# Maxima of the first attention unit's last two key chunks taken as one tile plus the relu of a difference, with the negated queries on ScalarE's side and three value projections moved later

## The chip, the cores and the metric

The kernel runs on one core of a Trainium2 chip. The metric is the device time of one execution in microseconds, as the median of three runs. Engines are named PE (TensorE), DVE (VectorE), ACT (ScalarE), POOL (GpSimd) and SP (SyncE, here only a queue that issues DMAs).

## The reference

Two transformer layers on 2048 tokens of width 128, each an attention and a feed-forward part behind a modulated layer norm. The change touches only the attention of the first layer, whose core is:

```python
q = (x @ Wq.T + bq).reshape(b, s, 16, 8)          # s = 2048, 16 heads of 8
k = (x @ Wk.T + bk).reshape(b, s, 16, 8)
v = (x @ Wv.T + bv).reshape(b, s, 16, 8)
w = jnp.einsum('bshd,bzhd->bhsz', q, k) / jnp.sqrt(8)
w = jax.nn.softmax(w, axis=-1)                    # subtracts each row's maximum over all 2048 keys
vw = jnp.einsum('bhsz,bzhd->bshd', w, v)
x = x + ga * (vw.reshape(b, s, 128) @ Wo.T + bo)
```

Behind it come the routed feed-forward part of layer 0, and layer 1 with causal attention over 8 heads of 16 and a gated mixing step.

## The kernel before

**Staging.** Layer 0's attention runs in 16 units, layer 1's in 8. A unit of layer 0 is one chunk of 512 queries (`CH`) and one quad of 4 heads. It has two parts. The first makes the row maxima: for each of 4 query tiles `qt` (128 queries), 2 pairs of heads `pair` and 4 key chunks `kb` of 512 keys, one score tile `s` is made, 32 in all. PE writes the pair's two halves of 128x512 into a double bank, `S0` and `S1` in turn (L985, two matmuls of 24 rows each, since q and k are held as three half-precision parts of 8). DVE reduces the 128x1024 numbers to two maxima in `mx` (L1377) and gives the bank back. When a unit's 32 tiles are done, DVE takes the maximum over the four chunks and negates it (`neg`, `nm`, L1385), POOL splits it in two half-precision parts (L1925 to L1929), PE turns it (`neg_turn`, L1008), ACT copies it to `nrow` (L1622), and four DMAs put it as two more rows beside the queries (L2078).

The second part needs these rows: for each of 16 tiles of 128 keys (a step), PE makes the transposed scores with the maximum subtracted (`st`, L1024, 26 rows, banks `T0` to `T2` in turn), ACT takes the exponential (L1637) and PE multiplies by the values (`pv`, L1059). In the steady state the score tiles of the next unit are made beside the steps of the present one, two tiles a step.

**The first unit** has nothing before it to hide behind. Its score tiles run in the order of the key chunks (`score_tiles`: `kb` outermost), since the chunks of k are still being projected, split into parts, written to DRAM and loaded back in the other layout (`project`, `split`, `load`; stores L2037 and L2038, loads L2051, all issued by SP in the order written). Call these tiles 0 to 31: tile 16 is the first of chunk 2, tile 24 the first of chunk 3. Then come seven tiles of unit 1, and only then the first step. Between the tiles PE does the remaining projections of q (L943), the modulation `mod` (L889, twelve matmuls of one column), the value projections `values` (L965, four of them, each copied by ACT at L1605 into `Va`), and matmuls of ones whose result nobody reads, `keep_busy` (L912).

**What sets the order.** `make_plan` writes one list of stages by hand and by rules; every engine walks this list and does what concerns it, in that order, with semaphore waits. `next_t` deals out `T0`, `T1`, `T2` in turn, `next_s` deals out `S0`, `S1`. A bank is opened by PE only when its last reader has freed it. `rows_in` makes PE wait for the loads of the k and q chunk. ACT's queue is strictly in order too: a `split` of q needs the shared buffer `qf` and its parts, which are free only when the DMAs that store an earlier chunk's parts are done.

## Time and profile before

| what | value |
|---|---|
| three runs | 1031.02, 1036.03 and 1037.11 us, median 1036.03 |
| profiled execution, its own time | 1036.88 us |
| its span from the first to the last instruction | 1035.1 us |
| mean granted clock of PE | 0.964 of full speed |
| busy, PE / DVE / ACT / POOL | 965.8 / 876.2 / 810.9 / 220.6 us |
| chain that ended last | PE 53%, DVE 30%, ACT 6% |
| largest line of that chain | DVE mx L1377, 26% of the span |

The profile is one execution. "Busy" adds up instructions, and the busy time of PE is modelled, since matmuls are pipelined. Two instructions of one kind may overlap by some 80 ns in it, so the pace of a row of them is read from their starts. A row of the timeline may merge several like instructions: it gives the first start, the time from there to the last end, and the count. The granted clock is the share of 2.4 GHz at which PE was let run: 1.00 or 0.50 (1.2 GHz).

### The profile page before, as it was taken

To read this page: it belongs to the slowest core of one execution; us is meant where nothing else is said; L and a number is where in the kernel's file an instruction comes from. 1 tells how busy PE (TensorE), PEld (TensorE's weight loads), DVE (VectorE), ACT (ScalarE), POOL (GpSimd) and SP (SyncE) were. 2 spreads that over 40 slices of the span, in tenths; PEclk is the share of its full clock that TensorE was granted. 3 is DMA by queue.
4 is the path that set the end of the run, shared out by engine and by line. 5 is a ranking of instruction groups with operands and counts; after the bars stand their busy time and mean duration, and the time that the engine had idled before them with its cause. 6 is when DMAs were issued, how large, how long until landed. Compare 5 with 4: busy or idle time off the path is not lost.

```text
span 1035.1 us, 23103 instructions
## 1 busy us (share of the span) xinstructions
PE 965.8 (93%) x9342; PEld 363.7 (35%) x9342; DVE 876.2 (85%) x1123; ACT 810.9 (78%) x1627; POOL 220.6 (21%) x395
## 2 busy tenths in 40 slices
PE   5999999999999999999999799989998999888988
PEld 2542322233333333333333145423333464332324
DVE  7999999999999999999999788853578777889704
ACT  4149999998999988999998588765774577667886
POOL 4233300003121103221203400141032312301112
PEclk9889999999999999999999789987899999999999
DMA  3520400000000000000000263112100441100000
GB/s 102 172 54 3 138 17 17 2 2 2 2 2 2 2 2 2 1 3 2 2 2 2 70 196 94 41 38 56 37 3 1 122 112 43 47 12 2 1 12 11
DMA packets 41387, 37.05 MB, mean 36 GB/s; under 512 B 5085, under 2 KB 39453, under 8 KB 41281
## 3 DMA queue, kind: packets, MB, share of 16 engines
q1 hardware_dynamic: 39024, 30.20, 10.1%
q0 software_dynamic: 1824, 5.25, 1.8%
q8 instruction: 73, 1.20, 0.5%
q14 instruction: 34, 0.27, 0.1%
q10 hardware_dynamic: 432, 0.13, 0.1%
HBM read 21.92 MB, written 13.30 MB: 34 GB/s over the span
## 4 chain that ended last, share of the span: by engine, by line
PE 53%; DVE 30%; issue 7%; ACT 6%; POOL 2%; DMA 1%; another core or an unknown queue 0%; ACTq 0%; DVEq 0%; POOLq 0%; SPq 0%
DVE mx L1377 26%; PE O L1059 20%; PE T L1024 11%; ACT PT L1637 2%; PE S L993 2%; PE T L1138 2%; PE T L1035 2%; PE S L985 1%; ACT PT L1631 1%; PE S L1189 1%; POOL XP L1994 1%; PE S L998 1%; PE T L943 1%; PE O L912 1%; PE T L1145 1%
## 5 line engine op out<-in xcount | busy, mean ns | idle before, releaser
L1377 DVE TENSOR_REDUCE mx<-S 128x2 f32<-128x1024 f32 (+2 forms) x672 | 755.1, 1179 | 56.6 <-PE S L998 21.3
L1637 ACT ACTIVATE PT<-T 128x512 f32<-128x512 f32 (+2 forms) x1280 | 657.8, 585 | 96.3 <-PE T L1024 41.1
L1059 PE MATMUL O<-PT,Va 128*9 128x256 f32 (+1 forms) x4040 | 337.2, 395 | 4.5 <-ACT Os L1671 4.5
L1024 PE MATMUL T<-Qs,Ks 26*128 26x512 f16 x1024 | 242.9, 394 | 11.9 <-ACT PT L1637 6.3
L985 PE MATMUL S<-Ks,Qs 24*128 24x512 f16 x1024 | 202.7, 394 | 8.1 <-DVE mx L1377 6.0
L1024 PEld LDWEIGHTS T<-Qs,Ks 26*128 26x128 f16 x1024 | 68.0, 91 | 232.1 <-issue 136.3
L1059 PEld LDWEIGHTS O<-PT,Va 128*9 128x9 f32 x4040 | 67.6, 88 | 125.4 <-issue 111.0
L1059 PE MATMUL O<-PT,V 128*17 128x256 f32 (+2 forms) x984 | 83.3, 406 | 1.2 <-ACT Os L1671 0.9
L993 PE MATMUL S<-K,Qs 48*128 48x512 f16 (+3 forms) x320 | 60.1, 359 | 11.7 <-DVE mx L1377 9.8
L985 PEld LDWEIGHTS S<-Ks,Qs 24*128 24x128 f16 x1024 | 48.2, 91 | 31.8 <-DVE mx L1377 24.9
L1035 PE MATMUL T<-Qs,K 50*128 50x512 f16 (+3 forms) x256 | 51.0, 356 | 5.3 <-ACT PT L1637 3.9
L1825 POOL TENSOR_SCALAR_AFFINE_SELECT PT<-PT 128x256 f32<-128x256 f32 x64 | 26.3, 418 | 119.4 <-ACT PT L1637 92.8
L1925 POOL TENSOR_SCALAR n<-nm 128x16 f16<-128x16 f32 x24 | 6.4, 265 | 175.1 <-DVE nm L1385 174.9
L1977 POOL TENSOR_TENSOR gates<-gates 128x256 f32<-128x256 f32 x16 | 11.6, 727 | 136.3 <-ACT gates L1723 136.3
L1938 POOL TENSOR_TENSOR vw<-om,rl 128x128 f32<-128x128 f32 x16 | 6.5, 406 | 128.4 <-DVE rl L1391 128.4
L1035 PEld LDWEIGHTS T<-Qs,K 50*128 50x128 f16 x256 | 14.2, 93 | 44.9 <-issue 27.9
L1059 PEld LDWEIGHTS O<-PT,V 128*17 128x17 f32 x984 | 16.8, 95 | 35.0 <-issue 26.4
L1631 ACT ACTIVATE PT<-S 128x1024 f32<-128x1024 f32 (+3 forms) x32 | 27.7, 945 | 1.2 <-PE S L1035 1.2
L993 PEld LDWEIGHTS S<-K,Qs 48*128 48x128 f16 x320 | 15.8, 94 | 34.8 <-DVE mx L1377 24.1
L1622 ACT ACTIVATE nrow<-T 8x512 f16<-8x512 f16 x24 | 14.0, 584 | 12.8 <-PE T L1008 12.4
L1994 POOL DMA_INDIRECT XP<-sorted_y,posu x16 | 16.3, 1017 | 36.1 <-DMA sorted_y<-Vf 31.9
L1340 DVE RECIPROCAL rl<-O 128x4 f32<-128x4 f32 x3 | 0.5, 183 | 24.1 <-PE O L1095 24.0
(338 smaller groups left out, 892.8 us busy)
## 6 DMA issues: line engine op xcount, KB each, us to landing
Wg<-in_L_ffn_experts SPq DMA_DIRECT2D x28, 192.0 KB, 2.6
Ks<-in_L_ffn_experts SPq DMA_DIRECT2D x20, 192.0 KB, 2.9
Vf<-sorted_x SPq DMA_DIRECT2D x12, 256.0 KB, 4.6
sorted_y<-Vf SPq DMA_DIRECT2D x12, 256.0 KB, 2.3
rows_q<-q SPq DMA_DIRECT2D x7, 256.0 KB, 2.4
sorted_x<-XP POOLq DMA_DIRECT2D x1, 1792.0 KB, 10.7
Qs<-nrow SPq DMA_DIRECT2D x96, 2.0 KB
Qs<-rows_q SPq DMA_DIRECT2D x8, 192.0 KB, 3.7
```

The lines of the kernel that those rows point to most:

```text
L985: m = e.matmul(two[:, i, :], Qs[r0:r0 + 24, quad, q0:q0 + 128], Ks[r0:r0 + 24, quad, CH * kb:CH * kb + CH], start=True, stop=True, tile_po ...
L993: m = e.matmul(two[:, i, 0:n], Q1[r0:r0 + 48, 2 * quad + pair, q0:q0 + 128], K1[r0:r0 + 48, CH * kb:CH * kb + n], start=True, stop=True, t ...
L1024: e.matmul(bank, Ks[r0:r0 + 26, quad, keys], Qs[r0:r0 + 26, quad, CH * c:CH * c + CH], start=True, stop=True, tile_position=(r0, 0)).then_ ...
L1035: m = e.matmul(bank[:, lo:CH], K1[r0:r0 + 50, keys], Q1[r0:r0 + 50, 2 * quad + pair, CH * c + lo:CH * c + CH], start=True, stop=True, tile ...
L1059: m = e.matmul(acc[32 * g:32 * g + d1, lo:hi], v, PT[(2 * j + g // 2) % 4][:, p0 + lo:p0 + hi], start=fresh, stop=True, skip_group_check=n ...
L1138: e.matmul(bank[:, 0:256], w[:, 128 * bl:128 * bl + 128], hc(c, 256 * half, 256 * half + 256), start=True, stop=True).then_inc(full, 1)
L1377: e.tensor_reduce(mx[:, u % 2, h0:h0 + 2, kb], two[:, :, 0:n], AX.X, ALU.max).then_inc(free, 1)
L1622: e.activation(nrow[:, U % 2, :], bank.bitcast(F16)[0:8, 0:CH], ACT.Copy).then_inc(free, 1)
L1631: e.activation(both, Sb[turn["st", L, j, 2 * pair][0]][:, :, lo:CH], ACT.Exp).then_inc(free, 1)
L1637: e.activation(PT[(2 * j + pair) % 4][:, CH * i + lo:CH * i + CH], bank[:, lo:CH], ACT.Exp).then_inc(free, 1)
L1825: e.affine_select(out=both, in_=both, compare_op=ALU.is_ge, fill=0.0, base=0, pattern=[[0, 2], [1, 128]], channel_multiplier=-1).then_inc( ...
L1994: e.indirect_dma_start(out=XP[:, t, :], out_offset=None, in_=sorted_y[g], in_offset=off(posu[:, t:t + 1])).then_inc(y_gathered[c], 16)
```

## The change

Only unit 0 is concerned (`FOLDED`). For each of its 8 pairs of `qt` and `pair`:

- the tile of chunk 3 is no longer made or reduced, so unit 0 has 24 score tiles, and the former tiles 24 to 31 are gone;
- a new stage `fold`, one for each head, makes on PE the difference of the scores of chunk 3 and chunk 2 in a `T` bank, by two accumulating matmuls on the same 24 rows: negated queries times chunk 2, plus queries times chunk 3. ACT writes the relu of it to SBUF (`relus`, four buffers of 128x2x512 in `Vf`);
- the tile of chunk 2 (tiles 16 to 23) is then not reduced by one instruction of 128x1024 but by two `tensor_tensor_reduce` of 128x512, which add tile and relu and take the maximum of the sum. max(a, b) = a + relu(b - a);
- chunk 1's reduction (tiles 8 to 15) reads the same 128x1024 numbers but writes two maxima for each head, over 256 keys each, so that the fourth column of `mx` is filled too.

A stage `negate` makes the negated queries by one ACT copy behind tile 12. A tile's two folds stand two tiles ahead of it in the list from tile 14 on. `mod` moves from behind tile 18 to behind tile 16, `values(0)` from behind tile 25 to behind tile 19, and `values(1)`, `(2)`, `(3)` from between the last tiles of unit 0 to behind the first, second and seventh tile of unit 1. Behind tiles 14 to 21 `keep_busy` has 2 matmuls where it had 8 or 4; in the section of unit 1 it has 6 in three places where it had 10. Nothing behind the first step moves on any engine, and SP and POOL keep their order throughout.

```diff
+FOLDED = {0: [(qt, pair) for qt in range(4) for pair in range(2)]}
...
-        return [(qt, pair, kb) for qt, kb in pairs for pair in (1, 0)]
+        return [(qt, pair, kb) for qt, kb in pairs for pair in (1, 0) if kb < 3 or (qt, pair) not in FOLDED.get(u, ())]
...
+        if is_folded(t):
+            for i in range(2):
+                fold(t, i)
         between("s", *t)
+        for t2 in tiles[si[0]:si[0] + (4 if u else 2)]:
+            if is_folded(t2) and t2 not in seen:
+                seen.add(t2)
+                for i in range(2):
+                    due.append(lambda t2=t2, i=i: fold(t2, i))
...
-        elif i == 18:
+        elif i == 16:
             beside("mod", 1)
-        elif i in (25, 27, 29, 31):
-            values((i - 25) // 2)
-        if 4 <= i < 25:
-            keep_busy(4 if i in (5, 7, 9, 11, 13, 15, 18) else 8)
+        elif i == 19:
+            values(0)
+        if i == 12:
+            negate(0)
+        if i >= 14:
+            while due:
+                due.pop(0)()
+        if 4 <= i < 22:
+            keep_busy(4 if i in (5, 7, 9, 11, 13) else 8 if i < 14 else 2)
     for i in range(7):
...
         emit_s()
+        if i in (0, 1, 6):
+            values(i + 1 if i < 2 else 3)
...
-        keep_busy(3 if i in (3, 4, 5) else 10 if i < 6 else 10)
+        keep_busy(3 if i in (3, 4, 5) else 6 if i in (0, 1, 6) else 10)
...
+                elif name == "fold":
+                    u, qt, pair, i = a
+                    c, quad = UNITS[0][u]
+                    bank, full = opened(("fold",) + tuple(a))
+                    rows_in(c, quad, 2)
+                    rows_in(c, quad, 3)
+                    pe.wait_ge(negated, P.negated[u])
+                    r0 = 64 * pair + 32 * i
+                    q0 = CH * c + 128 * qt
+                    e.matmul(bank, negs[r0:r0 + 24, u % 2, 128 * qt:128 * qt + 128], Ks[r0:r0 + 24, quad, 2 * CH:3 * CH], start=True, stop=False,
+                             tile_position=(r0, 0))
+                    e.matmul(bank, Qs[r0:r0 + 24, quad, q0:q0 + 128], Ks[r0:r0 + 24, quad, 3 * CH:4 * CH], start=False, stop=True,
+                             tile_position=(r0, 0)).then_inc(full, 1)
...
+                    if L == 0 and (qt, pair) in FOLDED.get(u, ()) and kb == 2:
+                        r = relus[P.folds[u, qt, pair] % 4]
+                        for i in range(2):
+                            done(("fold", u, qt, pair, i))
+                            m = e.tensor_tensor_reduce(r[:, i, :], two[:, i, :], r[:, i, :], 1.0, -3.0e38, ALU.add, ALU.max, mx[:, u % 2, h0 + i, 2:3])
+                        m.then_inc(free, 1)
+                        continue
+                    if L == 0 and (qt, pair) in FOLDED.get(u, ()) and kb == 1:
+                        e.tensor_reduce(mx[:, u % 2, h0:h0 + 2, 1:4:2], two[:, :, :].rearrange("p h (s n) -> p h s n", s=2), AX.X, ALU.max).then_inc(free, 1)
+                        continue
...
+                elif name == "fold":
+                    u, qt, pair, i = a
+                    bank, free = filled(("fold",) + tuple(a))
+                    n = P.folds[u, qt, pair]
+                    if n >= 4:
+                        u0, qt0, pair0 = fold_keys[n - 4]
+                        done(("s", 0, u0, qt0, pair0, 2))
+                    e.activation(relus[n % 4][:, i, :], bank, ACT.Relu).then_inc(free, 1)
+                elif name == "negate" and a[0] == 0:
+                    done(("pick", "q"))
+                    e.activation(negs[:, 0, :], Qs[:, 0, 0:CH], ACT.Copy, scale=-1.0).then_inc(negated, 1)
```

Three places show what moves. On PE, before, from tile 14 (the first row) to tile 16 (the last); T2 takes the second half of the q projection of chunk 3, and O the matmuls of ones:

```order
L985 MATMUL S0<-Ks,Qs 128x512 x2
L912 MATMUL O<-onesb 128x128 x8
L985 MATMUL S1<-Ks,Qs 128x512 x2
L943 MATMUL T2<-hT,wqT 128x256
L912 MATMUL O<-onesb 128x128 x4
L985 MATMUL S0<-Ks,Qs 128x512 x2
```

On PE, with the change, from the second fold of tile 16 (T1), which stands behind tile 14, to tile 16 (the last row); `Vf` holds the negated queries:

```order
L1052 MATMUL T1<-Ks,Vf 128x512
L1054 MATMUL T1<-Ks,Qs 128x512
L955 MATMUL O<-onesb 128x128 x2
L1028 MATMUL S1<-Ks,Qs 128x512 x2
L986 MATMUL T2<-hT,wqT 128x256
L1052 MATMUL T2<-Ks,Vf 128x512
L1054 MATMUL T2<-Ks,Qs 128x512
L1052 MATMUL T0<-Ks,Vf 128x512
L1054 MATMUL T0<-Ks,Qs 128x512
L955 MATMUL O<-onesb 128x128 x2
L1028 MATMUL S0<-Ks,Qs 128x512 x2
```

The folds of tile 17 now stand between the projection into T2 and tile 16, and the first of them is the next user of T2.

On ACT, before, the splits of the q chunks 2 (T1) and 3 (T2) and the first copy of values:

```order
L1596 ACTIVATE qf<-T1,bqs,sc 128x512
L1598 ACTIVATE q3<-qf 128x512
L1596 ACTIVATE qf<-T2,bqs,sc 128x512
L1598 ACTIVATE q3<-qf 128x512
L1605 ACTIVATE Va<-O 128x64x8
```

On ACT, with the change, the same place; `Vf<-Qs` is the negation and `Vf<-T0` and its like are relus:

```order
L1662 ACTIVATE qf<-T1,bqs,sc 128x512
L1664 ACTIVATE q3<-qf 128x512
L1791 ACTIVATE Vf<-Qs 128x512
L1788 ACTIVATE Vf<-T0 128x512
L1788 ACTIVATE Vf<-T1 128x512
L1662 ACTIVATE qf<-T2,bqs,sc 128x512
L1664 ACTIVATE q3<-qf 128x512
L1788 ACTIVATE Vf<-T2 128x512
L1788 ACTIVATE Vf<-T0 128x512
```

The relus of tile 16 stand ahead of the split of q chunk 3, those of tile 17 and all later ones behind it.

On PE at the end of the section of unit 1, before, from its fifth tile (the first row, S0) to the first step (T1 from `Ks` and `Qs`):

```order
L985 MATMUL S0<-Ks,Qs 128x512 x2
L898 MATMUL T2<-XP 128x128 x2
L912 MATMUL O<-onesb 128x128 x3
L985 MATMUL S1<-Ks,Qs 128x512 x2
L904 MATMUL T0<-XP 128x128 x2
L912 MATMUL O<-onesb 128x128 x3
L985 MATMUL S0<-Ks,Qs 128x512 x2
L912 MATMUL O<-onesb 128x128 x22
L1024 MATMUL T1<-Qs,Ks 128x512
```

With the change, from the sixth tile (S1) to the first step (T2):

```order
L1028 MATMUL S1<-Ks,Qs 128x512 x2
L947 MATMUL T1<-XP 128x128 x2
L955 MATMUL O<-onesb 128x128 x3
L1028 MATMUL S0<-Ks,Qs 128x512 x2
L1008 MATMUL T2<-wvT,hT 128x128 x4
L955 MATMUL O<-onesb 128x128 x18
L1080 MATMUL T2<-Qs,Ks 128x512
```

A value projection now stands ahead of the first step, and four of the twenty-two matmuls of ones are gone.

## Rows read from the trace of the kernel before

**Rows 1.** Busy time by window: stretch, length, busy us (instructions) by engine, clock, DMA.

```profile
20.00:40.00 20.00, 17.81 (x140) 9.77 (x141) 18.88 (x17) 7.11 (x11) 7.28 (x8) 1.00 0.50 160
40.00:60.00 20.00, 18.73 (x134) 12.27 (x131) 17.80 (x20) 3.38 (x6) 1.39 (x2) 0.74 0.28 87
...
110.00:200.00 90.00, 88.56 (x968) 26.51 (x960) 89.86 (x88) 86.23 (x169) 10.95 (x47) 1.00 0.16 46
```

**Rows 2.** Timeline, DVE in the first unit: start, us, instruction, count, idle before.

```profile
25.74 17.06 DVE L1377 TENSOR_REDUCE mx<-S 128x2 f32<-128x1024 f32 x15 [0.49 <-PE S L985]
...
53.63 6.88 DVE L1377 TENSOR_REDUCE mx<-S 128x2 f32<-128x1024 f32 x6 [1.32 <-PE S L985]
```

**Rows 3.** Timeline, DVE at the end of unit 0 and in unit 1.

```profile
60.54 0.22 DVE L1385 TENSOR_REDUCE nm<-mx 128x16 f32<-128x64 f32 x1
60.68 8.00 DVE L1377 TENSOR_REDUCE mx<-S 128x2 f32<-128x1024 f32 x7
...
68.86 5.75 DVE L1377 TENSOR_REDUCE mx<-S 128x2 f32<-128x1024 f32 x5 [0.17 <-PE S L985]
```

**Rows 4.** Busy time by window, the two low stretches of PE's clock.

```profile
44.40:54.40 10.00, 10.00 (x59) 6.37 (x59) 7.84 (x7) 0.60 (x1) 0.00 (x0) 0.50 0.26 76
...
71.00:72.00 1.00, 0.73 (x8) 0.22 (x10) 1.00 (x2) 0.86 (x2) 0.99 (x1) 0.76 0.92 327
72.00:73.00 1.00, 1.00 (x12) 0.11 (x4) 1.00 (x2) 0.00 (x0) 0.92 (x2) 0.50 1.12 328
...
74.00:75.00 1.00, 1.00 (x16) 0.24 (x12) 0.80 (x2) 0.57 (x2) 0.80 (x1) 0.53 0.39 66
```

**Rows 5.** DVE by line and shape: out<-in, count, busy us, mean ns, idle before.

```profile
L1441 DVE TENSOR_TENSOR Vf<-S,Vf 128x512 f32<-128x512 f32 x8 | 5.5, 691 | 0.5 <-PE S L1131 0.3
```

**Rows 6.** Timeline, ACT: an accumulator read between two activations, and exponentials.

```profile
6.02 0.19 ACT L1576 ACTIVATION_READ_ACCUMULATOR squares<-wkT 128x1 f32 x1
6.12 0.29 ACT L1576 ACTIVATE squares<-wqT 128x128 bf16<-128x128 f32 x1
...
77.10 12.94 ACT L1637 ACTIVATE PT<-T 128x512 f32<-128x512 f32 x24
```

**Rows 7.** Timeline, SP's queue and ACT around tile 16.

```profile
34.73 2.43 SPq L2051 DMA_DIRECT2D Ks<-rows_k  x6
...
37.63 0.47 SPq L2038 DMA_DIRECT2D rows_q<-q  x1
...
40.30 0.78 ACT L1596 ACTIVATE qf<-T,bqs,sc 128x512 f32<-128x512 f32 x1 [4.82 <-DMA rows_q<-q]
```

**Rows 8.** Timeline, PE: two fp16 matmuls of 512 columns, and what follows.

```profile
18.02 0.59 PE L958 MATMUL S<-PT,Vf 128*128 128x512 f16 x2
...
18.45 0.60 PE L930 MATMUL T<-idf,xh 128*128 128x128 f32 x4
```

**Rows 9.** Timeline, PE: `mod`; then tile, ones and values at half clock.

```profile
40.91 1.50 PE L889 MATMUL T<-cs,XP 128*128 128x1 f32 x12
...
45.91 0.61 PE L985 MATMUL S<-Ks,Qs 24*128 24x512 f16 x2
...
46.45 1.03 PE L912 MATMUL O<-onesb 128*128 128x128 bf16 x8
...
50.97 2.08 PE L965 MATMUL O<-wvT,hT 128*128 128x128 f32 x8
```

**Rows 10.** Timeline, PE: last value projection, then the end of unit 1's section.

```profile
58.62 1.16 PE L965 MATMUL T<-wvT,hT 128*128 128x128 f32 x8
...
59.72 0.39 PE L985 MATMUL S<-Ks,Qs 24*128 24x512 f16 x2
...
66.55 0.39 PE L985 MATMUL S<-Ks,Qs 24*128 24x512 f16 x2
...
66.87 1.40 PE L912 MATMUL O<-onesb 128*128 128x128 bf16 x22
...
68.21 0.40 PE L1024 MATMUL T<-Qs,Ks 26*128 26x512 f16 x3
```

More of the change, by code:

```diff
@@ L362, in make_plan @@
     out = dict.fromkeys(units, 0)
-    urgent = []
+    urgent, due, seen = [], [], set()
     si = [0]
@@ L379, in may_score, with is_folded, negate, fold @@
         return may_begin(*tiles[si[0]][:2])
+    def is_folded(t):
+        return t[0] == 0 and t[4] == 2 and t[2:4] in FOLDED.get(t[1], ())
+    def negate(u):
+        if u in FOLDED:
+            P.negated[u] = len(P.negated) + 1
+            P.stage("negate", u)
+    def fold(t, i):
+        key = t[1:4] + (i,)
+        if ("fold",) + key in P.turn:
+            return False
+        if i == 0:
+            P.folds[t[1:4]] = len(P.folds)
+        beside("fold", *key)
     def emit_s():
@@ L483, in do_later @@
     def do_later():
+        if due:
+            due.pop(0)()
+            return
         if urgent and urgent[0][0] <= now[0]:
@@ L739, in adaln_two_layers @@
         bsg, bt = Vf[:, 5632:5632 + CH], Vf[:, 6144:6144 + CH]
+        negs = Vf[:, 256:768].bitcast(F16).rearrange("p (k n) -> p k n", k=2)
+        relus = [Vf[:, o:o + 2 * CH].rearrange("p (i n) -> p i n", i=2) for o in (768, 1792, 5632, 6656)]
         pick = Vf[:, 0:256].bitcast(F16).rearrange("p (k s m) -> p k s m", k=2, s=2)
```

27 lines of the change are left out of this document (25 added, 2 removed).

## The prediction

> **What bounds the kernel now.** I read the busy times by window first. From 20 to 40 us DVE is busy for 18.88 us of 20, and in the steady state, 110 to 200 us, for 89.86 of 90, with PE at 88.56 and ACT at 86.23; in the first unit ACT has little to do, 3.38 us of the 20 behind 40 us [rows 1]. So ACT can take relus there, and whatever makes DVE end its share of the first unit earlier moves all that follows, since DVE has no free time behind it in which the gain could be lost.
>
> The timeline of DVE gives the pace: fifteen reductions in 17.06 us, 1.137 us each from start to start; the first of them is tile 4, so tile 15 starts at 38.25 and tile 16 at 39.39 [rows 2]. The last tile of unit 0 ends at 60.51 and `neg` starts at 60.54, the seven tiles of unit 1 follow at 1.143 each, and the eighth starts at 68.86 after only 0.17 us without work [rows 3]. The sixteen tiles that the change touches thus take from 39.39 to 60.54, 21.15 us, where sixteen times 1.137 is 18.2. The other 3 us are waits: PE ran at half its clock from 44.4 to 54.4, and DVE was busy for 7.84 of these 10 us only [rows 4].
>
> **What it removes and adds on DVE.** Sixteen reductions go, 18.2 us. Sixteen reduce-of-sum instructions of 128x512 come. The trace has none. Nearest is the sum of a PSUM and an SBUF source of 128x512 in single precision, 691 ns [rows 5]; a reduction of 1024 shows about 1.22 us where its pace is 1.137, so I take 0.61 as the pace. The order lists a second instruction behind each, which writes the accumulator. On ACT such a read takes 0.19 us, and the next instruction starts 0.10 after it [rows 6]; I take 0.10. A pair then costs 2 x 0.71 = 1.42 us, eight pairs 11.4. Bounds: with the read hidden 1.22 a pair; and at half rate, each half as dear as a whole reduction of 1024 plus the read, 2 x 1.24 = 2.48. I stay near the lower, since the row of the same two sources shows full rate. The reductions of chunk 1 keep their 1024 elements, and cost the same.
>
> A page of the Trainium skill speaks against the change here: Vector Engine (DVE) Microarchitecture Reference, Points that are easy to get wrong, says that the instruction family with two sources and an accumulator runs at half throughput if both sources are wider than bf16 and in SBUF. Here one source is in PSUM, so by its letter it does not apply; if it did, the sum would be that of the third rival. No row before has the accumulator.
>
> **What it adds on ACT and PE.** Sixteen relus of 128x512, each like the exponential of that size: 24 of them in 12.94 us, 0.54 each [rows 6]. A tile's two relus, 1.1 us, lie beside DVE's 1.42, and ACT was idle there. ScalarE: Activation LUTs, Rules for kernel authors, in the Trainium skill, would have a relu on VectorE; here VectorE is the engine that is waited for, and the trace disagrees with that advice.
>
> PE gets four matmuls of 512 columns for a tile. Two fp16 matmuls of that size took 18.02 to 18.45, 0.43 us [rows 8]: 0.86 for the two folds, and less if the two heads' row groups overlap. With the tile itself at 0.32 (66.55 to 66.87) and two ones at 0.06 each (22 in 1.40 us) PE needs 1.30 a tile at full clock [rows 10], under DVE's 1.42. At half clock the tile takes 0.54, the folds 1.72, the ones 0.26: 2.52 us [rows 9], far over it.
>
> **What is late next.** Two waits of the new folds lie on DVE's path.
> First, tile 16's folds stand ahead of tile 15 and need chunk 3 of k. Its four loads are the fifth to eighth of the twelve; the seventh starts at 34.73, the eighth is issued by 35.5. A store issued from 37.63 to 38.10 released ACT at 40.28, 2.2 us after its issue [rows 7]; so the rows are in at 37.7. Then 0.86 + 0.12, and tile 15 is issued at 38.7 and reduced from 39.1, 0.8 late.
> Second, and larger: tile 17's first fold needs bank T2, which holds the q projection of chunk 3 until ACT has read it, and ACT could start this only at 40.30, when the store had landed (0.78 us, to 41.08) [rows 7]. SP's order is unchanged, so that time stays. PE stands from about 39.7 to 41.1, and tile 16 is queued behind these folds: 41.1 + 0.98 = 42.1, its scores are in at 42.5. DVE's first pair starts at 42.5 instead of 39.39, 3.1 us late; the first wait is hidden in this.
> Then comes `mod`, 1.50 us on PE [rows 9], and tile 18's folds, ahead of tile 17: 42.4 + 1.5 + 0.98 = 44.9, scores at 45.3. Pair 16 ended at 43.9, so 1.4 us are lost, in which the copies of `mod` lie. Tiles 18 and 19 are issued at 46.2 and 47.5, in time. The value projection behind tile 19 takes 1.10 (58.62 to 59.72) [rows 10]; tile 20 is issued at 47.5 + 1.10 + 1.30 = 49.9 and its pair, due at 49.6, starts at 50.3: 0.7 lost.
>
> At full clock unit 0 would end at 42.5 + 11.4 + 1.4 + 0.7 = 56.0.
>
> **The clock.** The granted clock fell to half at 44.4, two us behind `mod`, whose matmuls have a single column, and came back at 54.4 [rows 4, 9]. With the change the same `mod` has a standstill of 1.4 us ahead of it, so I expect it to fall again. How long it stays low the rows show twice: 10 us, and some 3.4 us at 71.5 to 75 (0.24/0.5 + 2 + 0.94) [rows 4]. I take one short stretch: 3.4 us hold 1.35 tiles of 2.52 instead of 2.4 pairs of 1.42, 1.5 us lost, less 0.2 for PE's lead: 1.3. Unit 0 ends at 57.3, against 60.54: 3.2 us earlier.
>
> **Behind it.** Before, the first step came at 68.21, 7.7 behind the end of unit 0. The last tile of unit 1 waits for DVE as before, 6.0 behind; then 0.32, a value projection 1.10 and 18 ones 1.1 where 22 ones took 1.3 to 1.4: 8.5 [rows 10]. The first step and the eighth tile come 0.8 later relative to `neg`, and DVE, which had 0.17 us free [rows 3], stands for it. The other two value projections replace ones in a section that waits for DVE's 1.143 a tile, and cost nothing; without that cover 1.1 each. The copies on ACT lie in idle time.
>
> **Sum:** 3.2 - 0.8 = 2.4 us less. From the profiled execution's 1036.88 us that is 1034.5; its time is 0.85 above the median of the three runs, 1036.03, which would give 1033.6. I say 1034.
>
> **The rivals.**
> 1. *Larger gain.* The accumulator read costs nothing and the two heads' matmuls overlap (8 x 0.20 = 1.6), the clock stays up (1.3), and the ones at the end are covered by the DMAs of the maxima (0.8): 2.4 + 3.7 = 6.1 us, 1030.8. For it: PE is denser in the folds than it was with the ones. Against it: the standstill ahead of `mod`.
> 2. *Slower, because PE takes the bound at half clock.* If the clock is down from 44.4 to 54.4 as before, tiles 18 and 19 are issued at 47.4 and 49.9, tile 20 behind the values (2.0 [rows 9]) at 54.4, its pair starts at 55.0, and four pairs end at 60.7. With the 0.8 behind it the kernel is 1.0 us slower, 1037.9. If the clock stays down to the end of the unit, three more tiles at 2.52, a last 0.6 and a pair give 64.0: 4.3 us slower, 1041.2. It decides from about 8 us of low clock on, where 1.1 us lost a tile have eaten the gain. For it: that stretch before was that long, with PE at 10.00 of 10.00 us [rows 4]. Against: the second one was short.
> 3. *The reduce-of-sum runs at half rate.* Eight pairs of 2.48 from 42.5, with 0.3 for tile 17: 62.6, 2.1 later, and 0.8: 1039.8.
> 4. *It does nothing.* The end of the section is set by something that does not move, the rows of the maxima or the late loads behind them: these follow `neg` in SP's queue, so they move with it, and I give this little. 1036 to 1037.
>
> **How the numbers follow.** Forecast as above, 1032.5 to 1036.0: 0.50. Rival 1, 1029 to 1032.5: 0.20. Rival 2: 0.20. Rival 3: 0.05. Rival 4: 0.05. The three runs before already spread over 6 us, so the measured median adds 1 us either way. From 1029 to 1039 leaves out the far ends of rivals 1 to 3 and some of that spread, 2 in 10 at most; the likeliest case alone is 1032 to 1036.5. One per cent is 10.4 us, about what can be told from no change. Even pairs of 1.22 us without any wait behind the one for T2 would end unit 0 at 42.5 + 9.8 = 52.3, 8.2 us earlier, and miss it; the worst rival is at +5. So within 1%: 0.96, and 0.02 on each side for a state of the chip that no row shows.
>
> **What would show it.** Reduce-of-sum 0.65 to 0.75 us with a read behind it, a pair every 1.4 us; the first pair at 42.5, with PE waiting for T2 and ACT for the store of q; a granted clock of 0.50 for about 3.4 us within 43 to 50; `neg` at 57.3; the first step 8.5 behind it; from there on the same distances as before, and a span shorter by what `neg` gained less 0.8. It is wrong if the first pair starts near 39.4, if `neg` comes behind 60.5, or if a pair takes over 1.6 us.

## The result, and the profile after

The changed kernel takes 1043.9 us (median of 16 runs, 1037.6 to 1056.3), the kernel before 1037.0 in the same series (16 runs, 1031.0 to 1043.1): a ratio of 1.0071, with an interval of 1.0048 to 1.0094. It is slower by 0.7%, where I had said 1034 us and a range to 1039. The profiled execution took 1043.28 us, its span is 1041.5, and its mean granted clock 0.951 where that of before was 0.964. A ratio here and below leaves out a kernel's runs that lie over 1.5% above its fastest (one of the changed kernel's sixteen, and up to seven of twelve further down), while a median takes all of them, so the two can differ.

VectorE's timeline of the changed kernel (start, us, instruction, shapes, count, idle before and who ended it) answers [rows 2, 3]:

```profile
42.77 0.69 DVE L1437 CUSTOM_DVE_ANT_0 Vf<-S,Vf 128x512 f32<-128x512 f32 x1 [3.35 <-PE S L1028]
43.38 0.08 DVE L1437 DVE_READ_ACCUMULATOR2_ANT mx<- 128x1 f32 x1
43.38 0.69 DVE L1437 CUSTOM_DVE_ANT_0 Vf<-S,Vf 128x512 f32<-128x512 f32 x1
...
47.25 0.69 DVE L1437 CUSTOM_DVE_ANT_0 Vf<-S,Vf 128x512 f32<-128x512 f32 x1 [1.34 <-PE S L1028]
...
48.97 0.69 DVE L1437 CUSTOM_DVE_ANT_0 Vf<-S,Vf 128x512 f32<-128x512 f32 x1 [0.41 <-PE S L1028]
...
54.53 0.69 DVE L1437 CUSTOM_DVE_ANT_0 Vf<-S,Vf 128x512 f32<-128x512 f32 x1 [2.53 <-PE S L1028]
...
60.54 0.22 DVE L1451 TENSOR_REDUCE nm<-mx 128x16 f32<-128x64 f32 x1
...
63.17 1.23 DVE L1443 TENSOR_REDUCE mx<-S 128x2 f32<-128x1024 f32 x1 [1.28 <-PE S L1028]
...
66.48 2.36 DVE L1443 TENSOR_REDUCE mx<-S 128x2 f32<-128x1024 f32 x2 [2.08 <-PE S L1028]
...
102.53 0.22 DVE L1451 TENSOR_REDUCE nm<-mx 128x16 f32<-128x64 f32 x1
```

The first pair starts at 42.77 and then DVE waits for PE ahead of almost every pair. The maxima of unit 0 (`nm`) come at 60.54, to the hundredth where they came before [rows 3]: all that the folds save is eaten. Behind them stand two waits for unit 1's tiles, 1.28 and 2.08 us, where before seven tiles ran without one [rows 3].

PE's timeline shows why. The first rows are the last q projection (L986), first matmuls of folds (L1052) and `mod` (L932) in unit 0, then come the value projections (L1008), the ones (L955), the turned maxima (L1064, the transposition that unit 0's rows of maxima wait for) and the first step (L1080):

```profile
37.92 0.70 PE L986 MATMUL T<-hT,wqT 128*128 128x256 f32 x2
40.83 0.61 PE L1052 MATMUL T<-Ks,Vf 24*128 24x512 f16 x2 [2.20 <-ACT qf L1662]
...
42.66 2.72 PE L932 MATMUL T<-cs,XP 128*128 128x1 f32 x12
...
47.00 0.63 PE L1052 MATMUL T<-Ks,Vf 24*128 24x512 f16 x2
...
48.72 0.63 PE L1052 MATMUL T<-Ks,Vf 24*128 24x512 f16 x2
...
59.88 2.08 PE L1008 MATMUL T<-wvT,hT 128*128 128x128 f32 x8
61.74 0.85 PE L955 MATMUL O<-onesb 128*128 128x128 bf16 x6
...
63.06 1.54 PE L1008 MATMUL O<-wvT,hT 128*128 128x128 f32 x8
65.29 0.51 PE L955 MATMUL O<-onesb 128*128 128x128 bf16 x6 [0.69 <-ACT Va L1671]
65.73 0.39 PE L1064 MATMUL T<-idb,n 128*8 128x128 f16 x4
...
72.83 0.40 PE L1080 MATMUL T<-Qs,Ks 26*128 26x512 f16 x3
```

And the granted clock (window, its length, busy us and count of PE, PE's loads, DVE, ACT and POOL, clock, DMA share, GB/s), to set against [rows 4]:

```profile
39.00:40.00 1.00, 0.00 (x0) 0.00 (x0) 0.41 (x1) 0.01 (x1) 0.00 (x0) 1.00 0.65 171
40.00:41.00 1.00, 0.17 (x2) 0.13 (x4) 0.00 (x0) 0.97 (x2) 0.00 (x0) 0.50 0.77 258
...
63.00:64.00 1.00, 1.00 (x7) 0.94 (x6) 0.83 (x1) 0.00 (x0) 0.00 (x0) 0.56 0.00 0
64.00:65.00 1.00, 0.60 (x6) 0.41 (x4) 0.40 (x1) 0.36 (x1) 0.00 (x0) 1.00 0.00 0
```

The clock falls at 40.0, in the standstill that waits for bank T2, and comes back at 63.9: 23.9 us at half, where it was 10.2 in the profile of before. In that stretch a tile with its folds costs PE 1.72 us (47.00 to 48.72), more than the 1.22 of DVE's pair. The turned maxima come at 65.73 instead of 61.86, the first step at 72.83 instead of 68.21 [rows 10], and the maxima of unit 1 at 102.53 instead of 97.83: 4.7 us late. From the trace of before:

```profile
61.86 0.38 PE L1008 MATMUL T<-idb,n 128*8 128x128 f16 x4
```

```profile
97.83 0.22 DVE L1385 TENSOR_REDUCE nm<-mx 128x16 f32<-128x64 f32 x1
...
563.84 0.22 DVE L1385 TENSOR_REDUCE nm<-mx 128x16 f32<-128x64 f32 x1
...
615.92 0.22 DVE L1385 TENSOR_REDUCE nm<-mx 128x16 f32<-128x64 f32 x1
```

Up to unit 9 the lag stays within 4.4 and 4.7 us. But it does not reach the end unchanged. These are the maxima of units 13 and 14 in the changed kernel, beside the last two rows above:

```profile
571.22 0.22 DVE L1451 TENSOR_REDUCE nm<-mx 128x16 f32<-128x64 f32 x1
...
615.83 0.22 DVE L1451 TENSOR_REDUCE nm<-mx 128x16 f32<-128x64 f32 x1
```

The lag is 7.4 us at unit 13 and gone at unit 14, and at all maxima from there up to 765 us the two kernels lie within 0.7 us of each other. The 6.4 us between 1043.28 and 1036.88 come behind that, where low stretches of the clock differ again (17.1 us from 777 on in the change, 3.4 in before). So this one pair of profiles shows what the change does to the first unit and to unit 1, and can't show that this is what the medians differ by; for that see the timed runs below.

### The profile page after: what moved, and what is told of

Its sections match the earlier page's. It is cut to its first block, busy times and chain, and to the rows that moved or that the text cites. A ratio compares the mean times of both kernels' runs of the same rounds, so it can differ in the third digit from the quotient of the medians.

```text
span 1041.5 us, 23027 instructions
## 1 busy us (share of the span) xinstructions
PE 972.2 (93%) x9282; PEld 362.7 (35%) x9282; DVE 868.2 (83%) x1139; ACT 820.4 (79%) x1644; POOL 220.7 (21%) x395
## 4 chain that ended last, share of the span: by engine, by line
PE 55%; DVE 27%; issue 7%; ACT 6%; POOL 2%; DMA 2%; SPq 1%; ACTq 0%; DVEq 0%; POOLq 0%
DVE mx L1443 23%; PE O L1115 20%; PE T L1080 11%; PE S L1036 2%; ACT PT L1703 2%; PE T L1091 2%; PE T L1194 2%; PE S L1028 1%; ACT PT L1697 1%; PE S L1245 1%; PE S L1041 1%; POOL XP L2089 1%; PE S L1186 1%; PE T L986 1%; PE T L1201 1%
## 5 line engine op out<-in xcount | busy, mean ns | idle before, releaser
L1443 DVE TENSOR_REDUCE mx<-S 128x2 f32<-128x1024 f32 (+2 forms) x648 | 727.2, 1176 | 59.5 <-PE S L1041 23.4
L1080 PE MATMUL T<-Qs,Ks 26*128 26x512 f16 x1024 | 241.2, 394 | 4.0 <-ACT PT L1703 2.1
L1080 PEld LDWEIGHTS T<-Qs,Ks 26*128 26x128 f16 x1024 | 67.6, 91 | 222.3 <-issue 129.3
```

Of the source, the lines that this page charges most:

```text
L1080: e.matmul(bank, Ks[r0:r0 + 26, quad, keys], Qs[r0:r0 + 26, quad, CH * c:CH * c + CH], start=True, stop=True, tile_position=(r0, 0)).then_ ...
L1443: e.tensor_reduce(mx[:, u % 2, h0:h0 + 2, kb], two[:, :, 0:n], AX.X, ALU.max).then_inc(free, 1)
```

## The experiments

My two reasons were the half clock (theory C in the expectations: the standstill loses the clock and PE then bounds) and the value projections put ahead of the turned maxima (theory V). All sixteen further runs stand in this table: the low stretches of the clock that begin before 76 us (each widened to whole microseconds), the starts of unit 0's maxima, of the first step and of unit 1's maxima in the profiled execution, then the median and the ratio to the kernel before on the same chip. Runs with the same first letter shared a chip and the runs of before made there, whose medians were 1046.6 (e), 1044.4 (f), 1038.2 (g), 1045.2 (h) and 1044.5 (i); the first row and the second are the pair of the result.

| kernel | low, us | unit 0 | first step | unit 1 | median | ratio (interval) |
|---|---|---|---|---|---|---|
| before | 44-55, 71-75 | 60.54 | 68.21 | 97.83 | 1037.0 | |
| after | 40-64 | 60.54 | 72.83 | 102.53 | 1043.9 | 1.0071 (1.0048-1.0094) |
| e1 other bank | 37-62, 75-79 | 58.44 | 70.83 | 100.57 | 1057.9 | 1.0125 (1.0075-1.0176) |
| e2 more ones | 39-85 | 65.11 | 83.90 | 113.63 | 1059.6 | 1.0162 (1.0108-1.0215) |
| e3 folds only | 40-89 | 65.20 | 79.25 | 110.17 | 1051.9 | 1.0071 (1.0040-1.0102) |
| e4 values only | 41-66 | 61.83 | 74.20 | 103.90 | 1049.0 | 1.0050 (1.0014-1.0087) |
| f1 ones in the wait | 45-74 | 56.76 | 74.44 | 103.49 | 1048.0 | 1.0024 (0.9996-1.0052) |
| f2 held, values late | 43-64 | 60.86 | 72.25 | 101.30 | 1048.4 | 1.0030 (1.0002-1.0058) |
| f3 shallow ones | 40-61 | 61.82 | 69.49 | 98.63 | 1047.0 | 0.9962 (0.9913-1.0012) |
| f4 after again | 39-64 | 60.43 | 72.71 | 102.40 | 1051.2 | 1.0061 (1.0029-1.0094) |
| g1 half folded | 41-55, 58-73, 75-79 | 57.71 | 71.77 | 101.59 | 1040.8 | 1.0023 (0.9995-1.0051) |
| g2 values after the turn | 41-62, 75-79 | 59.30 | 70.64 | 100.39 | 1041.8 | 1.0054 (1.0020-1.0088) |
| g3 before again | 43-61, 74-78 | 61.96 | 69.63 | 99.38 | 1036.6 | 0.9989 (0.9955-1.0023) |
| h1 shallow opening | 41-62, 65-83 | 63.28 | 73.55 | 104.78 | 1049.6 | 1.0038 (1.0000-1.0076) |
| h2 before, more ones | 54-58, 71-75 | 59.00 | 66.67 | 96.44 | 1044.5 | 0.9971 (0.9927-1.0014) |
| h3 half, more ones | 68-72 | 56.18 | 64.72 | 94.36 | 1048.3 | 0.9979 (0.9929-1.0028) |
| i1 = h3 again | none | 56.24 | 64.78 | 93.83 | 1047.2 | 0.9940 (0.9883-0.9997) |
| i2 = h2 again | 69-76 | 58.27 | 65.93 | 96.78 | 1043.0 | 0.9985 (0.9947-1.0022) |

**The change taken apart (e).** e1 turns the banks by one, so that tile 17's folds need not wait for T2:

```diff
+        if i == 15:
+            P.next_t()
         if i >= 14:
             while due:
```

> The changed kernel with one T bank skipped in the deal, so that tile 17's first fold takes T0 and not T2, which the q projection holds until ACT's split at 40.0 us. In the changed kernel PE stood from 38.6 to 40.8 us there, DVE 3.35 us, and the clock went to half at 40.0 and came back at 63.6. Theory C (the loss is PE at half clock, set off by that standstill): without it tile 16 is issued near 39, the clock holds at least past 44, neg comes at 56 to 58 instead of 60.5, the first step at 65 to 68 instead of 72.8; 4 to 8 us faster than the changed kernel, level with the kernel before or better. Theory V (the loss is the value projections that now stand ahead of neg_turn, whatever the clock): neg comes earlier, but neg_turn still comes about 4 us later behind it than before; at most 3 us of gain. Rival: mod alone, 1.5 us of one-column matmuls, takes the clock down a few us later all the same; then the gain is only the 3 us of the standstill.

e2 gives the folded tiles 8 ones instead of 2:

```diff
-            keep_busy(4 if i in (5, 7, 9, 11, 13) else 8 if i < 14 else 2)
+            keep_busy(4 if i in (5, 7, 9, 11, 13) else 8)
```

> The changed kernel with 8 matmuls of ones behind each of tiles 14 to 21 instead of 2. Theory C with too few ones as the reason why the clock stays low: it comes back between 47 and 54 instead of 63.6, the section of unit 1 runs at full clock, the first step comes 3 to 5 us earlier. If the number of ones has nothing to do with it: the clock stays low, each tile costs 6 x 0.13 = 0.8 us more on PE, which is the bound there, neg comes up to 6 us later, at 65 to 67, and the kernel is 4 to 6 us slower than the changed one. Theory V says nothing of the clock; neg_turn is late behind neg by the values in both cases.

e3 has the folds, with the value projections back between the last tiles of unit 0 (behind tiles 17, 19, 21, 23) and unit 1's section as before:

```diff
-        elif i == 19:
-            values(0)
+        elif i in (17, 19, 21, 23):
+            values((i - 17) // 2)
```

> The folds as in the changed kernel, but the four value projections stand inside unit 0, behind tiles 17, 19, 21 and 23, and the section of unit 1 is that of the kernel before, with its 10 and 12 matmuls of ones. Theory V: neg_turn follows neg in 1.4 us again (1.3 before, 5.2 in the change), the first step comes 7.7 behind neg; the two values at half clock cost 2 x 2.0 inside unit 0 instead, the part of them that PE's lead does not cover, so neg at 63 to 66 and the first step at 71 to 73: 0 to 2 us faster than the changed kernel. Theory C: the clock is low through unit 0 all the same, PE is the bound there at 1.72 us a tile, three more values of 2.0 put neg at 66.5 and the first step at 74, 1 to 2 us slower than the changed kernel.

e4 is the kernel before with three value projections moved as the change moves them, and no folds:

```diff
-        elif i in (25, 27, 29, 31):
-            values((i - 25) // 2)
+        elif i == 27:
+            values(0)
...
+        if i in (0, 1, 6):
+            values(i + 1 if i < 2 else 3)
```

> The kernel before, with all 32 tiles reduced as they were, and only the value projections moved: the first behind tile 27, the other three into the section of unit 1 as in the change, with its 6 ones in place of 10. Theory V: neg_turn waits on PE for two projections and, through the ones in bank O, for ACT's copy; at full clock 2 x 1.1 us and some 0.6, less what PE waited for neg anyway (1.3): neg_turn 1.5 to 2 later behind neg, the first step 2 to 3 later, 2 to 3 us slower than the kernel before. Theory C: at full clock the projections fit beside DVE's 1.143 us a tile, so within 1 us of the kernel before. If the clock is low at neg here too, up to 4 slower.

In e1 the standstill is gone, PE is busy throughout 38 to 40 us, and the clock is low all the same, from 37.9 us on and for 23.9 us. So that standstill neither starts the low stretch there nor keeps it up (a wait of 0.48 us for the loads of k is left ahead of 36.6), and C's forecast of a clock held past 44 us failed. The gain of 2.0 us at unit 1's maxima is what V and the rival allowed. e2 and e3 do worse than the change: the clock stays low for 44 and 48 us, through the opening of unit 1. e2 did not bring the clock back sooner with four times the ones, and e3's first step at 79.25 lies 5 us and more behind the forecast of either theory. e4 has unit 1's maxima 6.1 us later than before (4.5 later than g3, a second profile of before) without a single fold. Both parts lose, each alone, though e4's profile has a low stretch of 23.9 us too and so does not price the moved projections at full clock.

The window of e3 behind unit 0, busy PE and yet at half clock:

```profile
56.00:76.00 20.00, 20.00 (x106) 12.04 (x105) 12.53 (x23) 5.64 (x10) 2.03 (x4) 0.50 0.05 10
```

**What the clock follows (f).** Theory S says the standstill, theory D the kind of matmul: the folds and tiles are 24 rows deep, the ones and value projections 128. Theory R says chance. f1 fills the standstill with ones:

```diff
+        if i == 15:
+            keep_busy(32)
         if i >= 14:
             while due:
```

> The changed kernel with 32 more ones matmuls (128 rows deep, some 1.7 us at full clock) put between the last q projection and the folds of tile 17, where TensorE stood still for 2.2 us. Theory S (the standstill costs the clock): TensorE stays at full clock past 43 us, the first unit's negated maxima come at 57 to 58 us instead of 60.5 and the ratio to the kernel before falls to 1.000 or below. Theory D (the folds, only 24 rows deep, in place of ones 128 rows deep cost the clock, whatever the standstill): the clock still falls somewhere in 37 to 48 us and stays low for 20 us or more, the negated maxima come at 60 us or later, ratio 1.005 to 1.015 as before. Theory R (chance of the single run): the low stretch is of any length, the ratio unchanged at 1.007.

f2 adds 6 ones behind each folded tile, and puts the values at tiles 2, 4 and 6:

```diff
-        if i in (0, 1, 6):
-            values(i + 1 if i < 2 else 3)
+        if i in (2, 4, 6):
+            values(i // 2)
```

> As the run with 32 ones in the wait, and besides 6 ones in place of 2 behind each folded tile (full-clock pace 1.26 us a tile against the 1.22 us of the pair), and the three late value projections behind the turned maxima (unit 1's tiles 2, 4 and 6) instead of tiles 0, 1 and 6. Theory S: full clock through the unit, maxima at 57 to 58 us, turned maxima 1.3 us behind them, first step at 65 to 66 us (68.2 before), ratio 0.997 to 0.999. Theory D: the added ones help part of the way; the clock is low for some 10 us as in the kernel before or for over 20; in the second case 1.005 to 1.015. Theory V (the values ahead of the turned maxima): whatever the clock, the turned maxima follow the negated maxima within 2.5 us instead of 5.2, and the ratio falls by about 0.002 to 0.003 against the changed kernel.

f3 is the kernel before with shallow ones in its first unit (a negative count from tile 14 on):

```diff
+                    rows = 128 if n > 0 else 24
-                    for _ in range(n):
-                        e.matmul(BANK[b][:, 0:128], onesb[:, :], onesb[:, :], start=True, stop=True)
+                    for _ in range(abs(n)):
+                        e.matmul(BANK[b][:, 0:128], onesb[0:rows, :], onesb[0:rows, :], start=True, stop=True)
```

> The kernel before, with the 8 or 4 ones matmuls behind each of the first unit's tiles 14 to 24 taken over 24 rows instead of 128: the same columns, the same TensorE time, nothing else changed (these matmuls compute nothing that is used). Theory D (the depth of what TensorE runs is what matters): the low stretch gets longer than the 10 us of before, over 20 us, and the time rises by 0.5 to 1.5%. Theory S and theory R: nothing changes, 1.000 within 0.003.

> The changed kernel once more, for a second profile. Theories S and D: the low stretch of the first unit starts at about 40 us and lasts over 20 us again, the ratio is 1.007. Theory R: it may last 3 to 10 us, with the maxima at 58 us, in this execution.

f4 repeats the change: 23.9 us again, every start within 0.15 us, in both its profiles; theory R loses by that. (The rest of the execution is not repeated: f4's span is 1047.9 us, 6.4 more, with the same first unit.) f1 is the cleanest view of the gain that I had forecast, and of where it goes. DVE's timeline of f1:

```profile
56.76 0.22 DVE L1453 TENSOR_REDUCE nm<-mx 128x16 f32<-128x64 f32 x1
...
63.97 1.23 DVE L1445 TENSOR_REDUCE mx<-S 128x2 f32<-128x1024 f32 x1 [3.35 <-PE S L1030]
```

and PE's between the two:

```profile
59.28 2.08 PE L1010 MATMUL O<-wvT,hT 128*128 128x128 f32 x8
62.05 0.82 PE L957 MATMUL O<-onesb 128*128 128x128 bf16 x6 [0.69 <-ACT Va L1673]
```

The clock holds until 45.9, the mod products take 1.50 us again, and unit 0 ends at 56.76, 3.8 us earlier than before. S had forecast this, but it is not shown to be the reason: the 32 ones are 128 rows deep themselves, e1 lost the clock without that standstill, and D's forecast (a fall within 37 to 48 us, low for over 20) came true as well. Then the clock is low until 73.2, and a value projection of 2.08, half-speed ones and their wait for ACT's copy of bank O turn -3.8 into +5.7 at unit 1's maxima. f2 has the values behind the turned maxima, which come 2.24 us behind unit 0's, as V said. But its unit 0 ends at 60.86, where S said 57 to 58: the clock fell at 43.3, sooner than in f1, in spite of 6 ones for 2, and +3.5 is left at unit 1's maxima.

f3's forecast by theory D was wrong in time: not slower. Its clock was low for 20.5 us. Its window beside that of g3 (the same kernel with deep ones):

```profile
44.00:52.00 8.00, 8.00 (x70) 6.57 (x67) 7.49 (x11) 0.00 (x0) 0.00 (x0) 0.50 0.33 97
```

```profile
44.00:52.00 8.00, 8.00 (x53) 4.84 (x52) 6.88 (x7) 0.00 (x0) 0.00 (x0) 0.50 0.31 93
```

DVE was busy for 7.49 of these 8 us at half clock (6.88 with deep ones): the tiles' matmuls started beside the shallow ones instead of behind them, so PE held up DVE less. With 20.5 us of low clock each, f3's unit 0 ends at 61.82 and h1's (below, with deep ones there) at 63.28. For the clock f3 says nothing: the kernel before can be low for 17.1 us (g3), and in h1, whose code up to the end of unit 0 is that of before, the stretch is 20.5 us, as in f3. Depth of the ones is not shown as the reason for a long low stretch in unit 0.

**Half of it (g).** g1 folds the last two query tiles only, and keeps three value projections in unit 0. Its expectation says that the ones stay at 8, but they do so only up to tile 18; behind tiles 19 to 27 it has none, where before has 8 behind each of 19 to 24:

```diff
-FOLDED = {0: [(qt, pair) for qt in range(4) for pair in range(2)]}
+FOLDED = {0: [(qt, pair) for qt in (2, 3) for pair in range(2)]}
...
-        elif i == 19:
-            values(0)
+        elif i in (19, 23, 25):
+            values((i - 18) // 2 - (i > 19))
...
-        if 4 <= i < 22:
-            keep_busy(4 if i in (5, 7, 9, 11, 13) else 8 if i < 14 else 2)
+        if 4 <= i < 19:
+            keep_busy(4 if i in (5, 7, 9, 11, 13, 15, 16) else 8)
...
-        if i in (0, 1, 6):
-            values(i + 1 if i < 2 else 3)
+        if i == 6:
+            values(3)
```

> Only the last two of the four query tiles (4 of 8 pairs) are folded; the mod products stand behind tile 16 as in the change, the value projections of chunks 0 to 2 stay inside the first unit behind tiles 19, 23 and 25, only that of chunk 3 stands in the second unit (tile 6), and the ones stay at 8. VectorE loses 4 reductions of 1.13 us and has 4 pairs of 1.22 for 4 reductions: 4.2 us less. Theory D with the values (what the shallow folds do to the clock, and three values put ahead of the turned maxima, make the loss): the first unit's maxima come at 57 to 59 us, those of the second unit some 37 to 38 us later, so 95 to 97 us against 97.8 before and 102.5 after the change; ratio 0.996 to 0.999. Theory R (the loss is chance or anywhere else): ratio 1.005 to 1.008 like the change.

g2 is the change with the values at tiles 2, 4 and 6, as in f2, and nothing else.

> The changed kernel with nothing moved but the three late value projections: behind the second unit's tiles 2, 4 and 6 (behind the turned maxima) in place of tiles 0, 1 and 6, with so many ones fewer there. If the values ahead of the turned maxima cost 2.3 us, the first unit's maxima stand at 60.5 us as in the change, the turned maxima within 3 us of them in place of 5.2, the second unit's maxima at 100 to 101 us in place of 102.5, and the ratio is 1.004 to 1.005 in place of 1.007. If their place doesn't matter (they take TensorE's time wherever they stand), the second unit's maxima stay at 102 to 103 us.

> The kernel before, unchanged, for a second profile and as a measure of what two runs of one kernel differ by. Theory D: the first unit's low stretch is short again (3 to 14 us), the maxima come at 60.5 us, the second unit's at 98 us, ratio 1.000 within 0.003. Theory R: the low stretch may be over 20 us here too, with maxima at 61 to 62 us and the second unit's at 100 us or later.

g1 gained 2.8 us in unit 0 and lost it: a second low stretch from 58.5 to 72.2 made the way from unit 0's maxima to the first step 14.1 us, where 7.7 is the rule. The loss moved with the clock, and the forecast of 95 to 97 us missed by 5. g2 shows that the place of the values, ahead of the turned maxima or behind, is a small part. The turned maxima come 2.23 us behind unit 0's (61.53 by PE's timeline, 5.19 in the change), yet unit 1's come 41.1 behind and not 37.3 (42.0 in the change): 0.9 us is the order, the rest is the work itself. It is not the half clock either: in g2 the clock was back at 61.9, and from the turned maxima at 61.53 to the first step at 70.64 it took 9.11 us where before takes 6.35. So three projections in this section cost 2.8 us with PE at full clock for nearly all of it. g3 differs from the first profile of before by 1.5 us in unit 1's maxima, with 17.1 us of low clock against a forecast of 3 to 14, and its own ratio is 0.9989.

**What a low clock costs, by place, and whether more deep work holds it (h, i).** h1 is the kernel before with shallow ones in unit 1's section only; h2 is before with more ones in unit 0; h3 is g1 with more ones. In the last two the edit is the list of counts, first h2's against before, then h3's against the change:

```diff
-            keep_busy(4 if i in (5, 7, 9, 11, 13, 15, 18) else 8)
+            keep_busy(4 if i in (5, 7, 9, 11, 13) else 8 if i < 14 else 6 if i == 15 else 14 if i == 18 else 10)
```

```diff
-        if 4 <= i < 22:
-            keep_busy(4 if i in (5, 7, 9, 11, 13) else 8 if i < 14 else 2)
+        if 4 <= i < 28:
+            keep_busy(4 if i in (5, 7, 9, 11, 13) else 8 if i < 14 else 6 if i == 15 else 14 if i == 16 else 10 if i < 19 else 0 if i in (19, 25) else 4)
```

> The kernel before, with the ones matmuls between the second unit's first seven tiles and the 12 behind them taken over 24 rows instead of 128 (they compute nothing that is used; nothing else changes). Theory P (the price is paid where TensorE bounds: a low clock in the first steps behind the maxima costs, one inside the first unit hardly does): the clock falls between 60 and 80 us, the first unit's maxima stay at 60.5 to 62 us, the second unit's come 40 to 44 us behind them instead of 37.3, ratio 1.003 to 1.008. Rival: the price doesn't depend on the place; with 10 us of low clock more it is 1.003 whichever section, and the distance between the two units' maxima stays below 39 us if the clock holds.

> The kernel before with more ones in the first unit: 10 instead of 8 behind tiles 14 to 24, 6 instead of 4 at tile 15, 14 instead of 4 behind the mod products. If 128-row work keeps the clock: the low stretch of the first unit (10.2 and 17.1 us in the two profiles of before) shrinks to 0 to 7 us, the maxima come at 58 to 60 us, ratio 0.995 to 0.999. If it doesn't, the added ones (0.13 us more a tile at half clock) cost 1 to 2 us: ratio 1.001 to 1.003.

> The half-folded kernel with more ones: 10 behind tiles 14 to 18, 6 at tile 15, 14 behind the mod products, 4 behind the folded tiles and the last ones (none where a value projection stands in their bank). If 128-row work keeps the clock, the second low stretch (58 to 73 us in the half-folded kernel's profile) goes, the first unit's maxima come at 56 to 58 us, the second's at 94 to 97 us, and the ratio is 0.995 to 0.999, better than both kernels. If not, the maxima come at 58 to 60 us and the ratio is 1.002 to 1.006.

> The half-folded kernel with more ones, unchanged, once more. Its first profile had the whole first unit at full clock, maxima at 56.2 us and the second unit's at 94.4 us (97.8 and 99.4 in the two profiles of before), and a ratio of 0.998 with 1 inside its interval. If the first unit's clock is held by the 128-row work, it is held again (low for 0 to 7 us before 75 us), the second unit's maxima come at 94 to 96 us and the ratio is 0.996 to 0.999. If it was chance, 10 to 24 us of low clock stand before 75 us and the ratio is 1.000 to 1.004.

> The kernel before with more ones, unchanged, once more. Its first profile had 3.4 us of low clock in the first unit (10.2 and 17.1 in the two of before) and its ratio was 0.997 with 1 inside its interval. If more 128-row work holds the clock: 0 to 7 us low again, the first maxima at 58 to 60 us, ratio 0.996 to 0.999. If it was chance: 10 to 20 us low, maxima at 61 to 63 us, ratio 1.000 to 1.003.

h1: 17.1 us of low clock behind unit 0's maxima, where before has 3.4, make the distance to unit 1's 41.5 us and not 37.3: 0.31 us for each further microsecond of low clock. That is theory P's forecast for this place. Inside the first unit the price is hardly lower. Up to the end of unit 0 before, g3 and h1 are the same kernel, and their 10.2, 17.1 and 20.5 us of low clock go with maxima at 60.54, 61.96 and 63.28: 0.27 us for each microsecond. So P's contrast between the two places falls.

With more ones the clock is low in unit 0 for 3.4 us (h2), 0 (i2), 0 (h3) and 0 (i1), against 10.2, 17.1 and 20.5 in the three profiles of before's first unit and 13.6 in g1, which has 13.7 more right behind it. That is the clearest effect of the ones here. It is not their number alone: from tile 14 to the end of unit 0 before has 80, h2 110, h3 78, the change 16, and e2 has 64 and f2 80 with low stretches of 44.4 and 20.5 us. h2 and h3 also have 14 ones behind `mod` where before has 4; which of the added ones matter was not tried. h3 and i1 hold the clock through unit 0, i1 up to 241 us. Two windows of i1, and its maxima:

```profile
36.00:56.00 20.00, 18.69 (x176) 11.64 (x173) 17.98 (x32) 7.37 (x13) 1.81 (x3) 1.00 0.41 126
56.00:76.00 20.00, 18.39 (x187) 9.04 (x184) 18.91 (x19) 11.93 (x24) 11.95 (x16) 1.00 0.27 71
```

```profile
56.24 0.22 DVE L1451 TENSOR_REDUCE nm<-mx 128x16 f32<-128x64 f32 x1
...
93.83 0.22 DVE L1451 TENSOR_REDUCE nm<-mx 128x16 f32<-128x64 f32 x1
```

Unit 1's maxima at 94.36 and 93.83, 3.5 to 5.6 us earlier than in the two profiles of before: half folding does gain where PE runs at full clock. At the end nothing certain is left of it. The profile of h3 ends at 1046.0 us. Behind 765 us, one stretch of half clock lasted 17 us in it, as in i1, h2, i2, f2, g2, h1, the change and f4, and 3.4 or 6.8 us in the two of before. In i1 the lead of 3.8 us holds up to 765 us and is a lag of 0.7 at the next maxima, behind that stretch. But such a stretch does not make a long profile by itself: g2 has it too, and with a span of 1034.8 us is the shortest of all. The medians of h3 and i1 are 1048.3 and 1047.2, both above those of before, the ratios 0.9979 and 0.9940; i1's rests on five runs. I can't call either kernel faster. h2 and i2 (0.9971, 0.9985) are not distinguished from before.

**The timed runs.** The ratios go with what the profiles show at unit 1's maxima. Of the thirteen rows with later maxima than before, eleven have a ratio above 1 (f3 and g3, with the two smallest lags, have not); of the four with earlier ones, all four are below 1, if three of them with 1 inside the interval. A straight line through the seventeen rows gives 0.95 us of time for each us at unit 1's maxima, with a correlation of 0.80. So the lag made in the first two units does reach the timed runs on the whole, though single kernels are off it by up to 11 us (e1).

Each timed run lists its mean granted clock. Over the 35 runs of before beside the f kernels, the time goes from 1038.9 us at 0.965 to 1058.9 at 0.940: 8 us for 0.01. The median clock there was 0.957, that of f4 (the change) 0.949: 0.008 less, by that price 6.4 us, of the 6.8 that its median lies higher. In e1 it was 0.939 against 0.954, 12 us by the same price, measured 11.3. So e1's single profile (span 1035.7, the lowest of its seven runs) says little of the whole kernel; its other runs have clocks of 0.920 to 0.945. Where in the program the missing clock of the timed runs lies they don't say.

## Why the prediction was wrong, step by step

- *Reduce-of-sum 0.71 with its read, 1.42 a pair.* It measured 0.61 from start to start, with the read of 0.08 hidden: 1.22 a pair, the lower bound. Rival 3, half rate, fell. The Trainium skill's sentence on two SBUF sources (Vector Engine (DVE) Microarchitecture Reference, Points that are easy to get wrong) asks for both sources in SBUF; one is in PSUM here, and the 0.61 us agree with its not applying.
- *Relus on ACT, 1.1 us a tile.* Right: 1.09 for two. ACT was never what DVE waited for.
- *The folds on PE, 1.30 a tile, 2.52 at half clock.* The two heads' matmuls overlap. At half clock it was 1.72; at full clock f1 shows 1.28 (from the tile at 43.89 to the next at 45.17). Sized too dear at half clock, and it did not help, since 1.72 is still above 1.22.
- *The wait for T2: the first pair at 42.5.* Measured 42.77, with ACT's copy at 39.99 behind the store. Right.
- *The clock: "I take one short stretch", 3.4 us, 1.3 lost.* This step failed. It was low for 23.9 us, in both profiles of the change. With the 1.72 a tile, `mod` at 2.72 instead of 1.50 and the value projection at 2.08, unit 0 ended at 60.54 and not at 57.3: all 3.2 us of the gain. I had the row that warned (10 us low with PE busy for all of them [rows 4]) and took the shorter of the two stretches without a reason. I did not ask what the change takes from PE's stream, 64 of the 80 ones from tile 14 on and three value projections, all 128 rows deep; that this is why the clock stayed low is suggested by h2, h3, i1 and i2, spoken against by e2, and not shown, since before's own first unit had 20.5 us once (h1). Rival 2 was this mechanism, at 0.20 and with `nm` at 60.7 to 64.0. That its lower end lies 0.2 from the measured 60.54 is luck: it had less than half the low stretch and a folded tile at 2.52 where 1.72 was measured. Its times, 1037.9 to 1041.2, are still too low.
- *"The other two value projections replace ones in a section that waits for DVE's 1.143 a tile, and cost nothing".* This step failed too. The turned maxima came 3.87 us late: 2.08 us for the first projection at half clock, the other in bank O with the ones behind it waiting 0.69 for ACT, and two tiles at half clock. The bank wait could have been read from the code. e4 shows the cost without any fold (the turned maxima 5.27 us behind unit 0's, before 1.32), and g2 shows that at full clock and behind the turned maxima three projections still cost 2.8 us up to the first step, where I had 0.8 for one and nothing for the other two. The last of them I had at +0.8, and between the turned maxima and the first step the change has 7.10 us for 6.35: 0.75. h3 and i1, with only that one in the section and at full clock, have 8.54 from maxima to first step against 7.67: 0.87.
- *Behind it, the same distances.* Right from unit 2 to unit 9, with +4.7 to +4.4. Behind that, the low stretches differ from execution to execution, and the lag goes and comes back.
- The sum was -3.2 + 0.8; measured up to unit 1 it was 0 + 4.7. The profiled executions differ by 6.4, which is close to the 6.9 of the medians by chance as much as by cause, since the pair was level at 765 us.

**What stays open.** What starts the low stretch in the first unit and what ends it: the standstill (S) and the depth of the matmuls (D) each have a run against them (e1; e2 and f2), and an effect of `mod`, behind or in which the clock fell in four profiles of before's first unit (before, g3, h1 and, with other values behind it, e4), was not tested alone. Why the long low stretch near 780 us comes in some kernels' profiles and not in others', and whether the first unit has a hand in it. Whether full folding with a held clock gains more than half of it: not tried. The part of each kernel's missing clock that lies behind 100 us in the timed runs.

## To carry to other kernels

Work that a kernel does only to keep an engine's clock up is part of its budget: a change that takes such matmuls out, or moves other deep ones elsewhere, should be costed at half clock for the whole section, and both sums belong in the forecast, not one as an aside. When a section is made faster for the engine that bounds it, ask first whether the next engine can follow at its slower clock. And judge by the mean granted clock of many runs: a single profile of e1 looked fast where the kernel was the second slowest of all.

## What was not expected of the hardware

- At half clock PE was shown busy for 20.00 of 20 us in e3 (56 to 76 us) and the clock did not come back; in the change it came back during the second of two value projections, 128 rows deep like the six ones between them. In h3 and i1, with more ones, it did not fall in unit 0; in e2, with more ones than the change, it stayed low for 44.4 us.
- Matmuls of 24 rows run beside each other: in the change at half clock the four matmuls of a tile's folds, on the rows of two heads, took 1.00 us (47.00 to 48.00), where two of 512 columns one behind the other take 0.43 at full clock [rows 8], so four would take 1.72 at half. In f3 the ones overlap the tiles.
- The same kernel's time moved by 8 us for 0.01 of mean clock, over 20 us between runs; that is more than the whole change.
- A reduce-of-sum of 128x512 shows 0.69 us, goes at 0.61, and its accumulator read of 0.08 costs nothing.
